# Linear layer in one program: output of the first batch beside features of the second, expert split spread anew

## The reference, cut to what matters

```python
q = x @ Wqk + bqk                       # k is the same
v = silu(x @ Wv + bv);  u = silu(x @ Wu + bu)
q = elu(heads(q));  kh = elu(heads(k))
kv = einsum('bhnd,bhne->bhde', kh, heads(v))      # over all 1024 rows of a batch
out = layernorm(einsum('bhnd,bhde->bhne', q, kv), ln_g, ln_b)
x = layernorm(x + (u * out) @ Wo + bo)
# then the router's logits, x @ gate_w.T, and the experts
```

## Time and profile before

| | us |
|---|---|
| median of 3 runs | 1742.95 |
| runs | 1738.2 to 1748.8 |
| profiled execution | 1737.88 |
| its span, first to last instruction | 1736.1 |
| mean granted PE clock | 0.973 of 2.4 GHz |

### The profile page before, as it was taken

The page is one execution under the profiler, slowest core; times in us unless marked ns, Lnnn a source line. Parts: engine busy times, 40 slices in busy tenths (PEclk is TensorE's granted clock), DMA queues, the critical chain, the costliest instruction groups (busy, mean ns, idle before and its releaser), DMA issues. The chain is left out here.

```text
span 1736.1 us, 33561 instructions
## 1 busy us (share of the span) xinstructions
PE 1582.6 (91%) x12554; PEld 802.2 (46%) x12554; DVE 1177.1 (68%) x2076; ACT 933.7 (54%) x1641; POOL 574.8 (33%) x581
## 2 busy tenths in 40 slices
PE   5899999899999987999979999687898899999997
PEld 3533333364333333444434444454565566666564
DVE  4599998458999964999866777796623243333387
ACT  5756777345677844777735665477232333333332
POOL 4556575171000021232222111496182111111265
PEclk9999999999999998999999999798999999999999
DMA  7422332000000011665548999562071765456344
GB/s 240 138 46 57 74 69 49 2 2 2 2 2 2 2 14 43 125 120 120 92 85 280 356 338 359 189 196 73 23 133 44 277 234 169 151 185 219 103 123 134
DMA packets 177841, 211.42 MB, mean 122 GB/s; under 512 B 114202, under 2 KB 117624, under 8 KB 175504
## 3 DMA queue, kind: packets, MB, share of 16 engines
q1 hardware_dynamic: 170336, 188.54, 36.3%
q0 software_dynamic: 7344, 20.73, 4.5%
HBM read 193.33 MB, written 56.40 MB: 144 GB/s over the span
## 5 line engine op out<-in xcount | busy, mean ns | idle before, releaser
L704 ACT ACTIVATE layer_scratch<-layer_banks 128x512 f32<-128x512 f32 x576 | 312.5, 595 | 136.4 <-PE layer_banks L601 134.9
L810 DVE TENSOR_REDUCE layer_mx<-layer_banks 128x2 f32<-128x1024 f32 (+3 forms) x304 | 339.2, 1155 | 24.1 <-PE layer_banks L579 20.6
L2202 PE MATMUL sparse_ps_g<-wgate,sparse_xT 128*128 128x352 f16 x1128 | 184.2, 313 | 1.6 <-DVE sparse_xT L2280 1.6
L616 PE MATMUL layer_banks<-layer_scratch,V 128*32 128x256 f32 x2304 | 174.6, 389 | 0.8 <-ACT layer_scratch L712 0.8
L1321 PE MATMUL lin_ps_z<-arena,early 128*128 128x512 f16 x576 | 134.9, 385 | 7.6 <-DVE lin_relu L1469 4.1
L2202 PEld LDWEIGHTS sparse_ps_g<-wgate,sparse_xT 128*128 128x128 f16 x1128 | 108.4, 98 | 62.0 <-DVE sparse_xT L2280 2.0
L2286 DVE SCALAR_TENSOR_TENSOR sparse_hid<-sparse_th,sparse_ps_g 128x352 f32<-128x352 f32 x47 | 24.5, 521 | 150.9 <-ACT sparse_th L2247 150.9
L2313 POOL DMA_INDIRECT xg<-x_d,token x45 | 42.5, 945 | 248.2 <-PE sparse_ps_x L2192 248.2
L1078 PE MATMUL ffn_ps_y<-wprojT,ffn_hT 128*128 128x512 f16 x512 | 115.6, 385 | 8.0 <-DMA ffn_hT<-ffn_h 8.0
L1068 PE MATMUL ffn_ps_fc<-wfcT,early 128*128 128x512 f16 x512 | 114.4, 382 | 5.8 <-PEq L934 3.4
L579 PE MATMUL layer_banks<-KT,arena 64*128 64x512 f16 (+3 forms) x768 | 113.8, 330 | 5.9 <-DVE layer_mx L810 5.8
(11 more groups left out here) (305 smaller groups left out, 3124.6 us busy)
## 6 DMA issues: line engine op xcount, KB each, us to landing
wgate<-gate_d SPq DMA_DIRECT2D x47, 1408.0 KB
wdown<-down_d SPq DMA_DIRECT2D x47, 768.0 KB
lin_sp_raw<-in_L_ffn_w_gate_up_dram SPq DMA_DIRECT2D x56, 352.0 KB, 5.3
gate_d<-lin_sp_parts SPq DMA_DIRECT2D x56, 352.0 KB, 5.0
y_d<-y SPq DMA_DIRECT2D x47, 256.0 KB, 4.9
down_d<-lin_sp_parts SPq DMA_DIRECT2D x42, 256.0 KB, 5.0
lin_sp_raw<-in_L_ffn_w_down_dram SPq DMA_DIRECT2D x28, 256.0 KB, 5.3
wfcT<-in_L_ffn_w_fc_dram SPq DMA_DIRECT2D x8, 512.0 KB, 7.1
```

The costliest lines, as they stand in the source:

```text
L616: last = pe.matmul(ps_o[32 * jj:32 * jj + 32, 256 * half:256 * half + 256], V[:, kt, 4 * jg + jj, :], prob[(2 * q + jj // 2) % 4][:, half, ...
L704: act.activation(prob[g % 4][:, par, :, :], ps_t[:, (2 * g + par) % 3, :, :], ACT.Exp, scale=HD ** -0.5).then_inc(exp_done, 1)
L810: dve.tensor_reduce(mx[x % 2][:, c, :, at:at + per], ps_s[:, 2 * (r % 2):2 * (r % 2) + 2, 0:per * n].rearrange("p e (h k) -> p e h k", k=n ...
L2202: last = pe.matmul(ps_g[u][n][rows, :], xT[u][:, a, k, rows], w, start=(k == 0 and i == 0), stop=(k == KC - 1 and i == 2), skip_group_chec ...
```

## The change

It does four things.

- `linear_features` and `linear_output_and_route` become one program, `linear_layer`. The output of tile t has its lag raised by `OUT_LAG` = 11: q of tile 0 is made in step 11, where the products of tile 9 are. Features run in steps 2 to 18, the output in steps 11 to 36; in steps 11 to 17 both work.
- All PSUM is shared out anew: z has two banks in place of three, so the third product of a tile waits for relu of the same tile; the turned x, q, w and y have one bank each in place of two. The subtraction moves ahead of gating, into the stage of the statistics. `m.U` is a ring of 11 tiles.
- The first expert's split moves into the ternary layer, a piece every second step, ring of 3. The other 15 and the shared one, 112 pieces, run in the linear layer with a ring of 4: four pieces at the end of each of steps 1 to 10; eight in each of steps 11 to 18, four in the middle of the step (`in_half(s, 0)`) and four at its end; two in each of steps 19 to 22.
- SP issues for each piece its store and then the load of the piece four later; after the first four loads it also loads the router's weights and tables. The experts' two tables in memory are declared earlier.

The diff, cut to its core:

```diff
 # ternary_ffn
+        split = ExpertSplit(f, m, d, 3, 0, FFN_EXPERTS, 0)
 # SP
+                unrolled(NT + AHEAD, [(0, of_layer(next_layer)), (3, xt), (3, split.every_second(split.load, sp)),
+                                      (5, of_layer(ht(0))), (5, of_layer(ht(1))), (7, split.every_second(split.store, sp))])
 # ACT, last in the list; DVE, last in the list
+                                      (5, split.every_second(split.high, act))])
+                                      (1, of_layer(x_norm)), (1, of_layer(next_low)), (5, split.every_second(split.low, dve))])

-LIN_EXPERTS = 14
+FFN_EXPERTS = 1
+OUT_LAG = 11
+URING = OUT_LAG

 # ExpertSplit
+    def in_half(self, s, half):
+        one, two, last = self.ring * (OUT_LAG - 1), 2 * self.ring, OUT_LAG + TB
+        if 1 <= s < OUT_LAG:
+            at, size = self.ring * (s - 1), self.ring * half
+        elif OUT_LAG <= s < last:
+            at, size = one + two * (s - OUT_LAG) + self.ring * half, self.ring
+        elif last <= s:
+            at, size = one + two * TB + 2 * (s - last), 2 * half
+        else:
+            at, size = 0, 0
+        return range(at, min(at + size, self.count))
+    def every_second(self, fn, eng):
+        def at(t):
+            if t % 2 == 0 and t // 2 < self.count:
+                fn(eng, t // 2)
+        return at

 # linear_layer
+        ps_x, ps_w = turns(0), turns(6)
+        ps_z = lambda t, i: banks[:, 1 + (3 * t + i) % 2, :]
+        split = ExpertSplit(f, m, d, 4, FFN_EXPERTS, NE - FFN_EXPERTS, 1)
 # SP
+                for i in range(split.ring):
+                    split.load(sp, i)
...
+                def pieces(s):
+                    for i in split.in_step(s):
+                        split.store(sp, i)
+                        if i + split.ring < split.count:
+                            split.load(sp, i + split.ring)
+                unrolled(NT + Q + 8, [(0, lambda s: rows(s - Q - 7)), (0, pieces)])
 # PE
+                def z(i):
+                    def fn(t):
+                        u = t % 2
+                        if i == 0:
+                            after(pe, xt_evac, t + 1 - AHEAD)
+                            after(pe, v_done, t)
+                        if i == 1:
+                            after(pe, u_done, t)
+                        if i == 2:
+                            pe.wait_ge(relu_done, t + 1)
...
+                unrolled(NT, [(1, xt), (Q + 3, wt), (2, z(0)), (Q, q), (2, z(1)), (Q + 4, wo), (2, z(2)), (3, kv), (3, router),
+                              (Q + 9, logit), (Q + 8, ot)])
 # ACT
+                unrolled(NT + Q + 9, [(0, of(lambda t: xhi(t + 1), 0)), (0, of(biases, 1)), (0, of(wevac, Q + 3)), (0, of(whi, Q + 2)), (0, of(exps, 2)),
+                                      (0, of(norm, Q + 6)), (0, of(ohi, Q + 6)), (0, pieces(0)), (0, of(tanhs, 2)), (0, of(kt_hi, 3)),
+                                      (0, of(kv_hi, 3)), (0, of(router, 4)), (0, of(oevac, Q + 8)), (0, pieces(1))])
 # DVE
+                unrolled(NT + Q + 10, [(0, of(residual, Q + 5)), (0, of(gating, Q + 1)), (0, of(xevac, 1)), (0, of(biases, 1)), (0, of(keys, 2)),
+                                       (0, of(stats, Q)), (0, pieces(0)), (0, of(values, 2)), (0, of(kt_lo, 3)), (0, of(kv_lo, 3)),
+                                       (0, of(router, 4)), (0, of(levac, Q + 9)), (0, pieces(1))])
 # POOL
+                unrolled(NT, [(0, xlo), (Q + 7, olo), (Q + 2, wlo), (Q + 5, root_r), (Q + 1, product), (2, minus_one),
+                              (Q, lambda t: ln_q.root(pool, t, t % 2))])
```

More of the change, by code:

```diff
@@ L1275, in store @@
                      self.parts[i % self.ring][:, 0:2 * width]).then_inc(self.stored[i % self.ring], 16)
[L1277 to L1284, removed]
     def wait_stored(self, sp):
@@ L1325, in biased, with linear_layer @@
     return pe.matmul(out, m.ones_row[:, :], m.bias[:, i, :], start=False, stop=True)
[L1328 removed]
+def linear_layer(nc, m, d):
     with Phase(nc, "lin") as f:
@@ L1402, in kv, with router, q @@
                     last.then_inc(kt_done, 1)
-                unrolled(NT, [(1, xt), (2, z), (3, kv)])
+                def router(t):
+                    if t == 0:
+                        pe.wait_ge(gate_in, 16)
+                        for k in range(KC):
+                            last = pe.transpose(ps_gate[:, k, :], gate[:, k * P:(k + 1) * P], m.ident[0:NE, 0:NE])
+                        last.then_inc(g_done, 1)
+                def q(t):
+                    if t % TB == 0:
+                        pe.wait_ge(kvl_done, 4 * (t // TB + 1))
+                    pe.wait_ge(ktl_done, t + 1)
+                    after(pe, n1_done, t)
+                    s = slice(t * P, (t + 1) * P)
+                    for g in range(KC):
+                        for n, (a, c) in enumerate(((0, 0), (0, 1), (1, 0))):
+                            last = pe.matmul(ps_q[:, g, :], m.kT[:, a, g, s], m.kv[:, t // TB, c, g, :], start=(n == 0), stop=(n == 2))
+                    last.then_inc(q_done, 1)
@@ new lines, in ot, with logit @@
+                def ot(t):
+                    pe.wait_ge(ol_done, t + 1)
+                    if t == 0:
+                        pe.wait_ge(xt_evac, NT - AHEAD)
+                    after(pe, ot_evac, t)
+                    transpose_parts(pe, ps_x, o2[t % 2], m).then_inc(ot_done, 1)
+                def logit(t):
+                    if t == 0:
+                        pe.wait_ge(ktl_done, NT)
+                    pe.wait_ge(ot_evac, t + 1)
+                    after(pe, l_evac, t)
+                    s = slice(t * P, (t + 1) * P)
+                    for k in range(KC):
+                        for n, (a, c) in enumerate(((0, 0), (0, 1), (1, 0), (1, 1))):
+                            last = pe.matmul(ps_l, m.xT3[:, a, k, s], gT[:, c, k, :],
+                                             start=(k == 0 and n == 0), stop=(k == KC - 1 and n == 3))
+                    last.then_inc(l_done, 1)
@@ L1442, in biases, with router @@
                         act.activation(m.bias[:, :, :], brow, ACT.Copy, scale=WS).then_inc(bh_done, 1)
-                unrolled(NT, [(0, lambda t: xhi(t + 1)), (1, biases), (2, nonlinear), (3, kt_hi), (3, kv_hi),
-                              (1, split.spread(split.high, act, NT, 3))])
+                def router(t):
+                    if t == 0:
+                        act.wait_ge(g_done, 1)
+                        act.activation(gT[:, 0, :, :], ps_gate, ACT.Copy, scale=WS).then_inc(gh_done, 1)
@@ new lines, in residual @@
+                def residual(t):
+                    u = t % 2
+                    dve.wait_ge(y_done, t + 1)
+                    after(dve, norm_done, t - 1)
+                    dve.scalar_tensor_tensor(r[u][:, :], ps_y, 1.0 / WS, m.X[:, t, :],
+                                             ALU.mult, ALU.add).then_inc(r_done, 1)
+                    dve.wait_ge(r_done, t + 1)
+                    ln_r.statistics(dve, r[u][:, None, :], t, u)
+                    dve.tensor_scalar(back[u][:, :], ln_r.mv[u][:, 0:1], -1.0, None, ALU.mult).then_inc(back_done, 1)
```

372 lines of the change are left out of this document (156 added, 216 removed).

## The result

The changed kernel takes 1790.7 us (median; 1788.0 to 1793.1), the kernel before 1741.8 beside it: a ratio of 1.0269, interval [1.0244, 1.0293]. It is slower, as forecast, but by 49 us and not by 10. The profiled execution has a span of 1786.2 us, 50.1 more than the one before.

A forecast was written before the change was run, and what follows sets the result against it. PE and DMA were both taken as full in the feature stretches, POOL fullest in the output. Start +7.0, interleaved steps +2.6 and three terms of 0 gave +9.6, called +10 us: median 1753 us, range 1737 to 1768.

The forecast's parts named there:

- the split's turnaround: Forecast's own case, steps 11 to 18: second batch waits for the four slots just freed; 1753 us, chance 0.48.
- Output from tile 8 on: Linear layer's output stretch from tile 8: same work and lags, so 67.0 us as before; 2 us less if POOL gains.
- Ternary layer: Seven pieces there fit into DVE's idle time and cost 0; 6.7 us if DVE becomes the bound.
- Start: Linear layer's first tile: two banks make the third product wait for relu; z(1) 4.3 to 7.6 us late, taken as 7.0.
- Steps 11 to 18: Interleaved steps, eight pieces each: 127.8 us together; with work before and behind +2.6 us, bounds -10.8 and +18.8.
- relu ahead of the third product: Sign that the forecast is right: in steps 11 to 18 PE idles before the third product, released by relu.
- 10.92 plus 0.7: PE's work in us per interleaved step, features plus q, so PE was not expected to set the step.
- Features alone: Tiles 1 to 8 of the linear layer: 87.4 us again, cost 0; 2.4 us if relu comes too late.
- PE waits for hT: Sign that the forecast is wrong: PE waiting for hT in the middle of the ternary layer.
- Wires: Rival, steps 11 to 18: DMA stays full and sets steps of 14.3 us; 1739 us, chance 0.25.
- DVE beside POOL: Rival: lows lengthened beside POOL's output work, 6 us, plus some of the ternary layer's 6.7; 1762 us, chance 0.20.
- Interleaving as intended: Rival: PE sets the interleaved steps, 97 us in place of 127.8; 1722 us, chance 0.07.

## Why the prediction was wrong

*Direction and reason: half right.* That the split's turnaround paces the interleaved steps, and so takes back what the merge saves, is shown by the ring of six. That the output from tile 8 on and the ternary layer cost nothing is not so: 27.8 of the 50 us lie there. The two terms that I had priced, the start and steps 11 to 18, came to 19.7 us where I had 9.6.

*Output from tile 8 on, "I take 67.0": the step that failed most,* +23.0 us. I carried the stage over because work and lags were the same, and checked POOL's list for it, not PE's. I had called POOL the fullest engine of the output stretches, and the earlier trace rows doesn't say so: DVE is, with 40.70 of 43.90 us, and then PE, with 53.77 of 67.00 against POOL's 53.52. The new order of PE, with `ot` and the logits last, stands in the diff. Followed through the waits it gives the loop of 10 us; moved back it gives 68.4.

*Steps 11 to 18, +2.6 forecast, +13.3 measured.* Mechanism right, one term too small: from the first store to the fourth piece on ACT I took 8.2 us, between 7.6 and 10.2; over the eight steps it was 8.5 to 10.9, 9.8 in the mean and 9.6 in the step shown. From the first low of the first batch to the last low of the second the eight steps took 98.1 us, where my sum has 8 x 10.9 = 87.1; that is 11.0 us, about the 10.4 by which they exceed my 127.8. The row had 10.2; I had argued it down because the queue would be empty. But SP issues store and load of one piece after the other, 0.9 to 1.0 us a pair in the step shown, so the fourth load goes out 3.5 to 4.5 us after the first store, and ACT has what it brings another 4.5 to 7.4 later. DVE's other work was 6.6 us in the step shown where I had 6.3, a small term. Of the signs that I had named, relu ahead of the third product is a small one of PE's waits there: 5.6 us in all, against 7.4 for v and 18.1 for the residual, which stands behind the second batch's lows. What I wrote of PE, "10.92 plus 0.7", is wrong from step 15 on, where `wo` and the transposes bring it to some 14.6; with four slots that stayed hidden.

*Start, +7.0 forecast, +6.4 measured:* right in size, and in the reason given first, two banks. Relu of the first tile and the products, in the kernel before and after:

```profile
910.78 10.71 PE L1321 MATMUL lin_ps_z<-arena,early 128*128 128x512 f16 x36 [3.46 <-PEq L1028]
...
924.37 0.69 DVE L1469 TENSOR_SCALAR lin_relu<-lin_ps_z 128x512 f32<-128x512 f32 x1 [1.07 <-ACT lin_e L1418]
```

```profile
916.14 8.05 PE L1330 MATMUL lin_banks<-arena,early 128*128 128x512 f16 x24 [3.45 <-PEq L1029]
...
931.55 4.60 PE L1330 MATMUL lin_banks<-arena,early 128*128 128x512 f16 x12 [4.82 <-DVE lin_relu L1620]
...
936.86 2.75 PE L1330 MATMUL lin_banks<-arena,early 128*128 128x512 f16 x12
```

```profile
930.80 0.69 DVE L1620 TENSOR_SCALAR lin_relu<-lin_banks 128x512 f32<-128x512 f32 x1 [1.48 <-ACT lin_e L1523]
```

Before, relu ended 14.3 us after the layer's start, and z(1) started with its end. Now it ends after 15.4, one high more being ahead of it: 1.1 us. The third product waits 4.82 us for it and takes 4.60, so that z(1) starts 5.4 us behind relu: 5.3 us more. A bank of its own wins only 1.5 us of that by itself (17.0 + 236.4 against 20.7 + 234.3), because z(1) then waits for v, 1.4 us behind relu, and the slow product moves into the next stage.

*Features alone, 0:* right, 87.6 against 87.4.

*Ternary layer, 0 with a bound of 6.7; measured +4.8.* I put the low into idle time that lies ahead of the instruction before it; an instruction queued behind a wait can't use that wait. PE waits for hT, which I had named as the sign, came at 796.91 and 838.99, and in the drain:

```profile
891.62 8.39 PE L1081 MATMUL ffn_ps_y<-wprojT,ffn_hT 128*128 128x512 f16 x32 [4.13 <-DMA ffn_hT<-ffn_h]
903.93 8.75 PE L1081 MATMUL ffn_ps_y<-wprojT,ffn_hT 128*128 128x512 f16 x32 [3.91 <-DMA ffn_hT<-ffn_h]
```

Before there was one such wait, 5.02 us, and 0.29 ahead of it.

*The rivals.* Wires: not in this kernel, DMA is at 0.83; with six slots they come close to setting the steps, and so does DVE, busy for 94%. DVE beside POOL: the lengthening is there, its price 2.9 us where I had 6. Interleaving as intended: not in this kernel, but once slots, order and spread are mended its mark appears, PE full in the interleaved steps (47.24 of 47.50 us, with DVE at 46.97 beside it). The layer is then 15.1 us shorter than before (287.6 against 302.7 by the stages), where that rival had 21.

*What stays open:* the part behind the layer was 522.6 us before and 524.7 to 539.0 in the profiles since, without an edit to its instructions (539.0 in the slowest of that kernel's seven executions); 2 us of the 50 may or may not belong to the change.

## What to carry to other kernels

When two loops are merged into one list per engine, don't carry a stage's time over because its work and lags are the same: follow each in-order list for one step and ask what now stands ahead of the instruction that frees a buffer. Turns of a ring are priced from the first store to the last arrival, with the issuing of every store and load in between, and a batch as large as the ring can't overlap its own turn. Idle time can hide new work only if it lies behind that work's place in the list.

## What the runs showed of the hardware

My floor for the wires, 346 GB/s at a DMA share of 0.96, was a mean over 87 us and no ceiling. The highest rate over 42 us of the linear layer is 367 GB/s in the kernel before and 382 in the run with six slots, at shares of 1.01 and 1.02:

```profile
1039.00:1081.00 42.00, 42.00 (x224) 20.80 (x224) 33.72 (x48) 25.48 (x42) 6.40 (x6) 1.00 1.01 367
```

```profile
1033.00:1075.00 42.00, 37.68 (x232) 19.62 (x230) 41.37 (x65) 26.46 (x43) 19.36 (x17) 1.00 1.02 382
```

The steps there took 12.6 to 13.9 us where I had 14.3 as the least; over all eight steps it is 13.9, only 3% less. In the kernel before PE was full too, so its mean rate was what the tiles asked for. A rate beside another full engine tells what was asked, not what the queue can carry. What it can carry is not shown by the run with six slots either, since DVE is busy there for 41.37 of 42 us.
